# Four graph layers in one kernel: the second layer's destination weights move from the node rows into the selection matrices

## The reference, cut to what is computed

```python
# layer 0: attention; score = exp(clip(K[src].Q[dst])), sums over the edges of a node
h_out = (wV / (Z + 1e-06)).reshape(n, H * D);  x = _layernorm(x + h_out)
# layer 1
deg = jnp.maximum(jnp.zeros((n,)).at[dst].add(1.0), 1.0)
edge_weight = (deg[src] * deg[dst]) ** (-0.5)
edge_msg = jax.nn.relu(edge_attr @ W1e + b1e) @ W2e + b2e
agg = jax.ops.segment_sum((x[src] + edge_msg) * edge_weight[:, None], dst)
combined = (1.0 + gin_eps) * x + agg
out = jax.nn.relu(combined @ W1n + b1n) @ W2n + b2n + x
x = _layernorm(x + out * rsqrt(mean(out * out) + RMS_EPS) * rms_w)
# layer 2: radial network of edge lengths, products with directions, sums over edges
# layer 3: softmax over the edges of each node, channel by channel
```

## Time and profile before

| | us |
|---|---|
| median of 3 runs (lowest to highest) | 4626.52 (4621.08 to 4627.65) |
| the profiled execution, and its span | 4619.58, 4614.9 |
| PE, DVE, ACT, POOL busy | 3700.7, 3313.9, 2856.1, 3271.2 |

### The profile page before, as it was taken

The page is one execution under the profiler, slowest core; times in us unless marked ns, Lnnn a source line. Parts: engine busy times, 40 slices in busy tenths (PEclk is TensorE's granted clock), DMA queues, the critical chain, the costliest instruction groups (busy, mean ns, idle before and its releaser), DMA issues.

```text
span 4614.9 us, 103452 instructions
## 1 busy us (share of the span) xinstructions
PE 3700.7 (80%) x25659; PEld 3147.4 (68%) x25659; DVE 3313.9 (72%) x7588; ACT 2856.1 (62%) x7389; POOL 3271.2 (71%) x3435
## 2 busy tenths in 40 slices
PE   6888888887376666666769888888888999999996
PEld 4555555555376666666658677677677888888886
DVE  4666666667554444444668777777787999999998
ACT  3777676766532222222357666666656888888886
POOL 4777777775677777777657777777747777777772
PEclk8898898888587777777879999999999999999998
DMA  7888888884443333333122222222228887888882
GB/s 231 246 234 239 236 233 239 236 236 146 112 100 76 82 81 77 82 77 81 42 62 57 57 56 56 56 56 57 56 76 243 236 235 234 235 235 234 234 235 77
DMA packets 645495, 677.23 MB, mean 147 GB/s; under 512 B 126761, under 2 KB 511295, under 8 KB 645247
## 3 DMA queue, kind: packets, MB, share of 16 engines
q0 software_dynamic: 133120, 327.79, 27.2%
q1 hardware_dynamic: 509838, 346.88, 25.1%
q10 hardware_dynamic: 2416, 1.18, 0.1%
HBM read 584.73 MB, written 89.08 MB: 146 GB/s over the span
## 4 chain that ended last, share of the span: by engine, by line
POOL 27%; issue 21%; PE 16%; DVE 12%; ACT 11%; DMA 7%; SPq 2%; ACTq 2%; DVEq 1%; POOLq 0%
POOL e_rows L852 19%; POOL xt L852 8%; PE banks L914 7%; DVE acc L938 5%; ACT e_away L891 4%; DMA xt<-up_t,e_index 3%; PE banks L1032 3%; DVE banks L1482 2%; ACT e_logit L1478 1%; ACT banks L1544 1%; DMA e_q_rows<-q_t 1%; DMA e_rows<-kv_t,e_index 1%; ACTq L944 1%; ACT e_rows L1543 1%; PE banks L437 1%
## 5 line engine op out<-in xcount | busy, mean ns | idle before, releaser
L938 DVE TENSOR_TENSOR acc<-acc,banks 128x256 f32 x3328 | 1383.3, 416 | 886.1 <-PE banks L914 749.3
L852 POOL DMA_INDIRECT xt<-up_t,e_index x800 | 757.3, 947 | 243.7 <-issue 213.0
L852 POOL DMA_INDIRECT e_rows<-x_t,e_index x772 | 730.3, 946 | 248.0 <-issue 232.8
L852 POOL DMA_INDIRECT e_rows<-fsv_t,e_index x772 | 730.1, 946 | 236.0 <-issue 217.9
L852 POOL DMA_INDIRECT e_rows<-kv_t,e_index x772 | 730.1, 946 | 235.3 <-issue 220.7
L1174 ACT ACTIVATE e_rows<-banks,e_rows 128x128 f32<-128x128 f32 x832 | 236.9, 370 | 726.5 <-DMA e_rows<-x_t,e_index 481.0
L914 PE MATMUL banks<-e_sel,e_msg 128*128 128x128 f32 (+1 forms) x3328 | 654.5, 312 | 0.0
L1165 PE MATMUL banks<-e_w,xt 65*128 65x128 f32 x1664 | 273.2, 317 | 350.8 <-DMA xt<-in_attr_rows 346.7
L914 PEld LDWEIGHTS banks<-e_sel,e_msg 128*128 128x128 f32 (+1 forms) x3328 | 356.3, 148 | 262.6 <-issue 171.3
L891 ACT ACTIVATE e_away<-node_iota,local 128x128 f32<-128x128 f32 x1664 | 526.0, 388 | 0.0
L1165 PEld LDWEIGHTS banks<-e_w,xt 65*128 65x128 f32 x1664 | 248.6, 229 | 359.5 <-issue 308.0
(11 more groups left out here) (193 smaller groups left out, 7046.3 us busy)
## 6 DMA issues: line engine op xcount, KB each, us to landing
e_q_rows<-q_t SPq DMA_DIRECT2D x832, 64.0 KB
sel_d<-e_sel_t SPq DMA_DIRECT2D x208, 256.0 KB
e_sel_t<-sel_d SPq DMA_DIRECT2D x208, 256.0 KB
e_far<-fdst_t SPq DMA_DIRECT2D x832, 64.0 KB
e_near<-near_d SPq DMA_DIRECT2D x208, 128.0 KB
xt<-in_attr_rows SPq DMA_DIRECT2D x208, 128.0 KB, 3.6
e_resets<-reset_d SPq DMA_DIRECT2D x208, 128.0 KB
xt<-up_t,e_index POOLq DMA_INDIRECT x800
```

Source lines behind the costliest of these rows:

```text
L852: G.indirect_dma_start(out=self.rows[:, u, i, 0:self.width], out_offset=None, in_=self.table, in_offset=bass.IndirectOffsetOnAxis(ap=index ...
L938: V.tensor_tensor(to, to, bank[n_bank][:, col:col + W].rearrange("p (k d) -> p k d", k=2), ALU.add).then_inc(self.s_added[i], 1)
```

## The change

**Second layer.** The source rows are stored as x + b2e with the inverse root in front, unscaled; ACT scales them by it after the gather (four more operations a group in `weighted`). The destination's inverse root now stands in the selection matrix: `after0` stores all inverse roots to `inv_t` in DRAM, SP loads for each chunk the 128 inverses from its base on, the same for all partitions (`load_inverses`, four DMAs of 64 KB a group, five groups of buffers), and DVE makes the selection in four instructions, equality times inverse. The first half of the sums begins at (1 + eps) x, turned: `after0` turns the normalised x and writes it scaled into `acc`, and POOL clears the second half there, so the clearing at the start of `edges1` goes. W2e times W1n is made once, and `after1` starts with two matmuls of 512 columns that read the sums where they lie.

**Everywhere.** Epsilon and factor go into ACT's square root, so DVE's L396 goes. Chunks past the last edge aren't gathered, and the last real one gathers its 10 rows.

**First phase.** Weights are loaded first and from ACT's queue, then x in the order of use, with the integers between; six streams instead of three; the tables are planned from 8 us and the blocks from 0; PE waits only for the weights it needs. In `after0` the score sums are turned in two parts, and there are six streams instead of seven.

The core of the diff:

```diff
@@ tables
+        load_w(0, "k", loaded_kv)
+        load_w(1, "v", loaded_kv)
+        load_b(0, "k", loaded_b)
+        load_b(1, "v", loaded_b)
+        load_w(2, "q", loaded_q)
+        load_b(2, "q", loaded_q)
         G.memset(x[:, FULL_TILES:, :], 0.0).then_inc(cleared_x, 1)
-        SP.wait_ge(cleared_x, 1)
-        SP.dma_start(x[0:REST, FULL_TILES, :], a["x"][FULL_TILES * P:N_NODES, :]).then_inc(loaded_x[-1], 16)
-        for n, name in enumerate(("k", "v", "q")):
-            A.dma_start(w_qkv[:, n * D:(n + 1) * D], a[f"L0_gnn_W{name}"]).then_inc(loaded_qkv, 16)
-            A.dma_start(b_qkv[:, n * D:(n + 1) * D], vec_row(a[f"L0_gnn_b{name}"])).then_inc(loaded_qkv, 16)
+        load_x(SP, 0)
+        load_x(SP, 1)
         wait(SP, m_ints)
         d_ints.did(SP.dma_start(ints[:, 0:whole, :], a["int_rows"][0:whole * P, :].rearrange("(q p) e -> p q e", p=P)))
         ints_in = d_ints.did(SP.dma_start(ints[0:rest, whole, :], a["int_rows"][whole * P:N_CHUNKS, :]))
+        load_x(SP, 2)
+        load_x(SP, 3)
+        SP.wait_ge(cleared_x, 1)
+        SP.dma_start(x[0:REST, FULL_TILES, :], a["x"][FULL_TILES * P:N_NODES, :]).then_inc(loaded_x[-1], 16)
...
+        d_out.did(SP.dma_start(inv_t[:, N_TILES * P:ROWS], zeros[0:1, :]))
@@ Stream.inverse_root
             col, root_of = (self.small[:, n, 0:self.size] for n in (0, 1))
-            yield V, 0.15
-            wait(V, *ready)
-            m = self.v.did(V.tensor_scalar(col, of, factor, eps, ALU.mult, ALU.add))
             yield A, 0.25
             self.enter(A)
-            wait(A, m)
-            m = self.act.did(A.activation(root_of, col, ACT.Sqrt))
+            wait(A, *ready)
+            m = self.act.did(A.activation(root_of, of, ACT.Sqrt, bias=eps[:], scale=factor))
@@ project0
-                    PE.wait_ge(loaded_qkv, 96)
+                    PE.wait_ge(loaded_kv, 32)
...
+        def queries(ctx):
+            for e in (PE, V):
+                e.wait_ge(loaded_q, 32)
+            own_made.append(project_own(ctx, w_qkv[:, 2 * D:], b_qkv[:, 2 * D:], q_t))
+
+        node_phase("proj0", make, 6, lambda ctx, closing: tables(ctx, closing, loaded_x, loaded_kv, loaded_b, loaded_q, made_ident, cleared_x),
+                   late=queries, also_begin=8.0)
@@ after0, sums_by_node
+            for tiles, of_tiles in ((slice(0, 2 * BLOCK), bank[6]), (slice(2 * BLOCK, N_TILES), bank[7])):
+                n = tiles.stop - tiles.start
+                turned = of_tiles[:, 0:n * (HEADS0 + 1)].rearrange("p (t h) -> p t h", h=HEADS0 + 1)
+                yield PE, 0.1 * (tiles.stop - tiles.start)
+                for t in range(tiles.start, tiles.stop):
+                    m = PE.transpose(turned[:, t - tiles.start, :], acc[0:HEADS0 + 1, 1, t * P:(t + 1) * P],
+                                     ident[0:HEADS0 + 1, 0:HEADS0 + 1])
+                m_turned = pe.did(m)
+                yield V, 0.1 + 0.06 * (tiles.stop - tiles.start)
+                wait(V, m_turned)
+                m = v.did(V.tensor_scalar(zs[:, tiles, :], turned[:, :, 0:HEADS0], 1e-6, None, ALU.add))
+                md.append(v.did(V.tensor_scalar(deg[:, tiles], turned[:, :, HEADS0], 1.0, None, ALU.max)))
+                wait(V, m)
+                inverse = v.did(V.reciprocal(zi[:, tiles, :], zs[:, tiles, :]))
+                per_node.append((tiles.stop, zi, inverse))
...
+            yield A, 0.6
+            wait(A, m)
+            with nc.allow_non_contiguous_dma(reason="one number of each node, once"):
+                d_inv.did(A.dma_start(inv_t[:, 0:N_TILES * P].rearrange("a (t p) -> p (a t)", p=P), inv_root_deg[:]))
             closing.append(m)
+            closing.append((d_inv, d_inv.at))
+            yield G, 6.0
+            wait(G, m_turned)
+            closing.append(g.did(G.memset(acc[:, 1, 0:N_TILES * P], 0.0)))
@@ after0, steps
-                m = k.g.did(G.tensor_tensor(t1[:, 0:k.size, 1:], x[:, k.own, :], tiles_of(b2e[:], k.size), ALU.add))
-                yield V, 0.2
-                k.rows_are_out(V)
-                wait(V, normed[0])
-                k.v.did(V.tensor_copy(t1[:, 0:k.size, 0:1], inv_root_deg[:, k.own].unsqueeze(2)))
-                yield A, 0.4 * k.size
-                wait(A, m, normed[0])
+                mg = k.g.did(G.tensor_tensor(t1[:, 0:k.size, 1:], x[:, k.own, :], tiles_of(b2e[:], k.size), ALU.add))
+                yield A, 0.2
+                wait(A, normed[0])
+                ma = k.act.did(A.activation(t1[:, 0:k.size, 0:1], inv_root_deg[:, k.own].unsqueeze(2), ACT.Copy))
+                yield SP, 0.4
+                wait(SP, mg, ma)
+                k.out.did(SP.dma_start(by_tile(x1_t)[:, k.own, :], sliced(t1, k)))
+                yield PE, 0.15 * k.size
+                wait(PE, normalized)
                 for j in range(k.size):
-                    m = k.act.did(A.activation(t1[:, j, 1:], t1[:, j, 1:], ACT.Copy,
-                                               scale=inv_root_deg[:, k.first + j:k.first + j + 1]))
-                yield SP, 0.4
-                wait(SP, m, (k.v, k.v.at))
-                k.out.did(SP.dma_start(by_tile(x1_t)[:, k.own, :], sliced(t1, k)))
+                    m = PE.transpose(k.bank[0][:, j * P:(j + 1) * P], x[:, k.first + j, :], ident[:])
+                m = k.pe.did(m)
+                yield A, 0.6
+                wait(A, m)
+                k.act.did(A.activation(summed_tiles(0, k.own), k.wide(0), ACT.Copy, scale=eps1[:]))
-        node_phase("after0", make, 7, sums_by_node)
+        node_phase("after0", make, 6, sums_by_node)
@@ after1
-                yield G, 1.4
-                mxe = k.g.did(G.tensor_scalar(sliced(sq, k), x[:, k.own, :], eps1[:], None, ALU.mult))
-                yield PE, 0.5 * k.size
+                nodes = slice(k.own.start * P, k.own.stop * P)
+                yield PE, 1.2
                 k.enter(PE)
-                for j in range(k.size):
-                    to = k.bank[0][:, j * P:(j + 1) * P]
-                    PE.matmul(to, summed_tile(0, k.first + j), ident[:], start=True, stop=False)
-                    m = PE.matmul(to, summed_tile(1, k.first + j), w2e[:], start=False, stop=True)
-                m = k.pe.did(m)
-                yield V, 0.2 * k.size
-                k.enter(V)
-                wait(V, m, mxe)
-                for j in range(k.size):
-                    m = k.v.did(V.scalar_tensor_tensor(out=z[:, j, :], in0=k.wide(0)[:, j, :],
-                                                       scalar=inv_root_deg[:, k.first + j:k.first + j + 1],
-                                                       in1=sq[:, j, :], op0=ALU.mult, op1=ALU.add))
-                ready = yield from k.transpose(lambda j: z[:, j, :], ht, 0, [m])
-                yield PE, 1.0
-                wait(PE, ready)
-                m = k.pe.did(PE.matmul(k.flat(1), w1n[:], sliced(ht, k).rearrange("p t d -> p (t d)"),
-                                       start=True, stop=True))
+                PE.matmul(k.flat(1), w1n[:], acc[:, 0, nodes], start=True, stop=False)
+                m = k.pe.did(PE.matmul(k.flat(1), w2e[:], acc[:, 1, nodes], start=False, stop=True))
                 yield A, 0.7
+                k.enter(A)
                 wait(A, m)
                 m = k.act.did(A.activation(sliced(h, k).rearrange("p t d -> p (t d)"), k.flat(1), ACT.Relu,
@@ EdgePass.gather
+    def edges_of(g, i):
+
+        return P if not isinstance(g.n, int) else min(P, max(0, N_EDGES - (g.n * GROUP + i) * P))
...
+                n = edges_of(g, i)
+                if not n:
+                    continue
+                index = self.index[0:n, at:at + 1] if from_ring else src_c[0:n, g.n * GROUP + i:g.n * GROUP + i + 1]
...
@@ edges1
-            ps = EdgePass(ctx, x1_t, D + 1, own=D, sels=2, sel=sel, fixed=
+            ps = EdgePass(ctx, x1_t, D + 1, own=D, sels=2, sel=sel, cleared=True, fixed=
...
+            INVS = 5
+            inv_dst = ps.sb("inv_dst", [P, INVS, GROUP, P])
+            s_inv = [ps.sem(f"inv{u}") for u in range(INVS)]
+
+            turned, joined = ps.sb("turned", [P, P]), ps.sem("joined")
+            PE.transpose(bank[6][:, 0:P], w2e[:], ident[:]).then_inc(joined, 1)
+            A.wait_ge(joined, 1)
+            A.activation(turned[:], bank[6][:, 0:P], ACT.Copy).then_inc(joined, 1)
+            PE.wait_ge(joined, 2)
+            PE.matmul(bank[6][:, P:2 * P], turned[:], w1n[:], start=True, stop=True).then_inc(joined, 1)
+            A.wait_ge(joined, 3)
+            A.activation(w2e[:], bank[6][:, P:2 * P], ACT.Copy).then_inc(joined, 1)
+            PE.wait_ge(joined, 4)
+
+            def load_inverses(g):
+
+                bases = ps.bases(g, SP_ENGINE)
+                if g.old(INVS):
+                    SP.wait_ge(ps.s_sel, g.upto(-INVS))
+                    carry(SP, ps.s_carry)
+                for i in range(GROUP):
+                    SP.dma_start(inv_dst[:, g.at(INVS), i, :], inv_t[:, ds(bases[i], P)].to_broadcast([P, P])
```

(13 more changed lines are left out.)

68 lines of the change are left out of this document (33 added, 35 removed).

## The result

The changed kernel is **slower**: 5015.1 us (median of four; 5007.9 to 5020.3) beside 4624.6 us (median of four; the three shown above gave 4626.5), ratio 1.0842 (95% interval 1.0829 to 1.0855). Its profiled execution has a span of 5006.3 us, the one of the kernel before 4614.9. Forecast was 4566, with 4537 to 4596 as the range. The case that came true is the one called "Slower", at 0.04, and it went further than that case's own figure of 4670.

What follows compares the result with a forecast made beforehand. POOL's gathers, 5.0 us a group, bound the second pass; DVE is 95% busy in the fourth. Savings 14.5 + 8 + 8 + 1 + 24 + 5 = 60.5 from 4619.6 give 4559; 6.9 for the median makes 4566 us, range 4537 to 4596.

Steps and rivals of the forecast that it cites:

- Slower: Rival, chance 0.04: SP bounds the second pass, deciding from 5.3 us a group; at 5.5 the kernel takes 4670 us.
- Loop of the second pass: Second edge pass: added ACT, DVE and SP work fits under POOL's 5.0 us a group; no change, bounds 0 and 10 us.
- signs of being wrong: Forecast is wrong if gathers spread, index waits grow, or the second node phase stays over 100 us.
- First phase: Before the first gather: earlier x lets PE begin at 7 to 9.5, gather near 44.5; 14.5 us less (10 to 17).
- the rival of 0.08: First phase, chance 0.08: new load order does nothing, PE starts at 17, gain 6 instead of 14.5; 4580 us.
- And so does the whole first pass: First edge pass: the whole pass moves earlier with the first phase's 14.5 us gain.
- First node phase: Between passes one and two: earlier DVE start 5.5 us, shorter middle 3, store costs 1; 8 us less (2 to 14).
- Start of the second pass: First gathers of pass two: clearing gone, radial work earlier, 7.3 us lost instead of 14.7; 8 us less.
- Second node phase: Between passes two and three: less PE and DVE work, 58 + 26 = 84 us; 24 us less (12 to 33).
- The rival of the clock: Second node phase, chance 0.17: PE mostly at low clock, phase 100 instead of 84, first node phase gains 2; 4588 us.
- Last two node phases: Third node phase 0.5 us less by the smaller root; last one 4.5 us less (1 to 7) without L396.
- Ends of the passes: Ends of edge passes: one gather of 832 goes, one has 10 rows; together 1 us less (0 to 3).

Runs made afterwards that it cites:

- own rows: Experiment 1: the changed kernel with each inverse load reading 128 different 512 B rows instead of one row for all partitions (output differs); 4578.9 us.
- experiment 14: The changed kernel with three of a group's four inverse loads reading 128 DRAM copies and the first still reading the shared row; 4594.7 us.
- experiment 11: The kernel before with only the changed first phase (load order, table start, six streams, queries waiting for their own weights); 4616.3 us, ratio 0.9988.
- experiments 9 and 10: Inverse roots stored turned, as 49 packets: in the changed kernel, 4994.8 us; with inverses in partition memory, clearing on VectorE and later broadcast, 4577.3 us.

## Why the prediction was wrong, point by point

**Loop of the second pass: forecast nothing (0 to +10), measured some 430 us more** (the pass with own rows beside the changed one). This is the step that failed, at the four loads of inverses, 2.5 us of the 3.3 that SP was given for a group. It priced an inverse load from the query loads of pass one, since size, number and queue are the same, and the row was right as far as it went: experiment 1 gives 1.89 us for four. What the row could not say is that a query load reads 128 different rows, and an inverse load one row 128 times. The mis-sized term is the four loads of a group: 1.9 us in the sum, 4.7 us in the mean (1.8 to 8.3) in the running pass, with which SP needs 7.0 us a group where 3.3 were forecast, and POOL waits for its indices. The rival "Slower" had the place, SP, and the point from which it decides (0.9 us a load, 5.3 us a group); it got 0.04 because the argument against it, six loads a group in pass one, counted loads and did not ask what they read. There was a warning in the diff, `to_broadcast([P, P])`, for which the trace of before has one relative only: `e_near` in pass one, one such load a group, of 1 KB for each partition; experiment 14 shows one of 512 B to be free at that distance. The bound upward should have been open, not 10 us. Two of the prediction's own signs of being wrong came true together: the gathers spread (7.0 us a group, not 5.0), and the waits for indices grew.

**First phase: forecast 14.5 less, measured 11.3** (9.4 to 11.4 in the runs). PE starts at 10.38, not at 7 to 9.5, waiting for x; from there to the end of the last addition it is 32.8 us, where 31.8 were forecast, and from that to the first gather 4.7, where 3.8 were. The order did what it says: the rival of 0.08 is out. These are PE, DVE and POOL in the timeline of the changed kernel:

```profile
10.38 1.94 PE L392 MATMUL banks<-ident,x 128*128 128x128 f32 x8 [10.38 <-DMA x<-in_x]
...
42.45 0.69 DVE L458 TENSOR_TENSOR proj_kv<-banks,b_sdv 128x512 f32<-128x512 f32 x1 [0.89 <-PE banks L451]
...
47.80 1.17 POOL L882 DMA_INDIRECT e_rows<-kv_t,src_c  x1 [34.78 <-issue]
```

**"And so does the whole first pass": measured 4.8 us (own rows) and 6.3 us (changed) lost by its end.** Not forecast at all; cause open (experiment 11).

**First node phase: forecast 8 less, measured 0.** The chain's start moved as expected: last addition to DVE's first product is 2.0 us (1117.07), where it was 8.7. The engines' work fell as expected too (DVE 39.6 to 33.0, ACT 37.1 to 32.9). The failed step is the store of single numbers, priced by ACT's queue time, for which 1 us was taken and 0.42 measured; its price was in the DMA engines that the blocks' stores need. With it mended, 4.4 and 6.3 us come out (experiments 9 and 10).

**Start of the second pass: forecast 8 less.** In the changed kernel it can't be read alone, as SP is already behind: POOL waits 19.7 us for indices there (12.6 before). With own rows it is 6.6 us from first to last gather, of which 1.25 are the gather that was left out; without loads 12.6. DVE's radial work begins 7.0 us after the first gather, as said. The two waits for indices are 3.9 and 6.3 us there, where 4.4 and 2.9 were forecast. Right in mechanism, 2 to 3 us too much.

**Second node phase: forecast 24 less, to 84; measured 22.0 less, 88.7.** The closest of the large steps, though by the prediction's own terms 84 from 110 is 26, and it took 24. PE 63.1 us busy where 58 was expected, DVE 57.9 for 54, and filling and draining 25.6 for 26. The rival of the clock (0.17, 100 us) is out: granted clock 0.84 for the phase, 0.86 before.

**Last two node phases: forecast 0.5 and 4.5 less, measured 1.4 and 4.6.** Right.

**Ends of the passes: forecast 1 less, measured 2.9 less in pass three, 2.3 to 2.7 more in pass four**, where DVE sets the pace. The second was not foreseen.

**The sum.** Against 4614.9 us of span, the kernel with own rows is 37.6 us shorter; forecast were 60.5. The missing 23 us are 5 of the first phase, 4.8 of pass one, 8.9 of the first node phase (0.9 longer there than before), 1.7 of the second pass and its ends, 3.3 of the second node phase and 2.7 of pass four, less small gains in pass three and after. So with loads of different rows the forecast would have been 13 us low, the time inside its range; with the shared row it is 449 us low. That it is 13 us and not 23 is luck: the forecast had 6.9 us added for the median of the kernel before, and the one run with own rows lies 1.6 us above its span, where the profiled run of before lies 4.7 above its own.

## What to carry to other kernels

Price a load by what it reads as well as by its size: where all partitions read the same few hundred bytes, and such loads follow each other, nothing measured on loads of different rows is a bound; put the table into the partitions' memory once, or make two copies. Price a transfer by its number of packets on the DMA engines, not by the issuing engine's time: a transpose and 49 rows beat 6272 single numbers. And when a wait names a transfer, look at what stands ahead of it in its queue before believing the name.

## What the runs showed of the hardware

A 64 KB load in which 128 partitions read one 512 B row takes some 1.5 us when such loads pile up (45 GB/s, an estimate from the 7.0 us a group), against 0.47 us of issue for one of 128 rows; with two copies (64 readers each) the price is hidden, and a lone one in 5 us issues in 0.33 us. Reading always the same row was a little slower still (first to last gather 1521.9 us for 1443.2, one run). A broadcast of 25.6 KB to each partition runs at 264 GB/s. That readers of one place are served one after the other, some 11 to 12 ns each (1.5 us by 128), would explain all of these. The queue's packets in the changed kernel come at that pace: here from 1714 to 1715 us, 84 of them.

```profile
q1 hardware_dynamic: 84, 0.04, 12.6%
```

With own rows 361 came in the microsecond from 1503.5. But the engines are only 13% busy with that queue in the slow microsecond, so whether packets are held up in the memory or before they reach the engines isn't shown; the one after the other remains the likeliest reading. A store of 6272 numbers of 4 B took 24.3 us and kept the DMA engines nine tenths busy for some 20 of them. In the changed kernel an inverse load took up to 3.25 us to issue on SP (0.33 us with own rows in the loop), and everything behind it on SP was late with it.
